# Attention scores and row maxima in five near-equal blocks of 460 or 462 columns instead of four of 512 and one of 256

## The reference

```python
attn = einsum('bqc,bkc->bqk', q * scale, k)          # 2304 x 2304 for each image and head
attn = attn + rel_h[..., :, None] + rel_w[..., None, :]   # relative position terms from q
attn = softmax(attn, axis=-1)
out = (attn @ v) @ proj_w + proj_b
x = x + out
```

## Time and profile before

| | |
|---|---|
| median of 3 runs | 6809.67 us (6804.43 to 6810.84) |
| profiled execution, span | 6801.4 us |
| PE busy / PEld busy | 6725.5 us (99%) / 4245.8 us (62%) |
| DVE busy | 5454.7 us (80%) |
| ACT busy | 4753.7 us (70%) |
| POOL busy | 938.1 us (14%) |
| DMA queue q1, share of the 16 engines | 68.9% |
| granted TensorE clock | full but for some slices' parts at the start and the end (2.4 GHz level) |

### The profile page before, as it was taken

One profiled execution on the slowest core, in us unless ns is written; L12 is line 12 of the kernel. 1 busy time (PEld: TensorE's weight loads), 2 busy tenths in 40 slices (PEclk: granted clock), 3 DMA queues, 4 the chain that ended last, 5 costly groups with the idle time before them and its releaser, 6 DMA issues.

```text
span 6801.4 us, 139326 instructions
## 1 busy us (share of the span) xinstructions
PE 6725.5 (99%) x53600; PEld 4245.8 (62%) x53600; DVE 5454.7 (80%) x9973; ACT 4753.7 (70%) x10225; POOL 938.1 (14%) x967
## 2 busy tenths in 40 slices
PE   7999999999999999999999999999999999999998
PEld 5666666666666666666665666666666666666664
DVE  7887888778887788877888778887888878888883
ACT  3776776767767777677776767767676676767775
POOL 2111010211112110121111210102101121101110
PEclk8999999999999999999999999999999999999999
DMA  6676676767677677667676766767677676777673
GB/s 164 148 156 152 137 160 138 163 151 142 152 144 168 144 143 156 149 158 149 142 155 149 158 143 143 161 145 166 140 144 157 147 165 138 143 152 156 144 154 88
DMA packets 306307, 1013.72 MB, mean 149 GB/s; under 512 B 107440, under 2 KB 196976, under 8 KB 215920
## 3 DMA queue, kind: packets, MB, share of 16 engines
q1 hardware_dynamic: 305648, 1004.81, 68.9%
HBM read 745.26 MB, written 255.69 MB: 147 GB/s over the span
## 4 chain that ended last, share of the span: by engine, by line
PE 96%; DMA 1%; DVE 1%; issue 0%; ACT 0%; SPq 0%; POOL 0%; DVEq 0%; ACTq 0%
PE work L805 30%; PE work L878 27%; PE work L796 27%; PE work L824 7%; PE work L843 3%; PE work L862 2%; PE work L851 1%; DMA moving<-rel_scratch 1%; DVE mpart L683 1%; PE work L830 0%; DVE xb L674 0%; ACT probs L561 0%; DMA back<-attention_scratch 0%; DVE hi L721 0%; PE work L835 0%
## 5 line engine op out<-in xcount | busy, mean ns | idle before, releaser
L683 DVE TENSOR_REDUCE mpart<-work 128x1 f32<-128x512 f32 (+1 forms) x8640 | 5088.7, 632 | 1079.7 <-PE work L805 1013.1
L561 ACT ACTIVATE probs<-work 128x512 f32<-128x512 f32 (+1 forms) x8640 | 4100.2, 564 | 866.6 <-PE work L796 852.1
L805 PE MATMUL work<-mkeys,hi 128*128 128x512 f32 (+1 forms) x8640 | 3404.1, 395 | 10.6 <-DVE mpart L683 8.8
L796 PE MATMUL work<-moving,keys 113*128 113x512 f32 (+1 forms) x8640 | 3299.9, 383 | 10.9 <-DMA moving<-rel_scratch 5.7
L805 PEld LDWEIGHTS work<-mkeys,hi 128*128 128x128 f32 x8640 | 1643.6, 190 | 622.4 <-DVE mpart L683 324.0
L878 PE MATMUL work<-probs,vall 128*17 128x288 f32 x27648 | 2013.1, 409 | 0.0
L796 PEld LDWEIGHTS work<-moving,keys 113*128 113x128 f32 x8640 | 1642.1, 190 | 362.3 <-ACT probs L561 39.2
L878 PEld LDWEIGHTS work<-probs,vall 128*17 128x17 f32 x27648 | 637.3, 96 | 846.8 <-ACT probs L561 358.3
L824 PEld LDWEIGHTS work<-image,tab 128*48 128x48 f32 x6912 | 401.6, 124 | 544.9 <-ACT probs L561 513.2
L490 POOL TENSOR_TENSOR full<-full,hi 128x384 f32<-128x384 f32 x576 | 583.5, 1016 | 938.7 <-DVE hi L721 937.6
L495 POOL TENSOR_TENSOR rden<-oraw,rden 128x576 f32<-128x576 f32 x96 | 137.1, 1428 | 3955.3 <-DMA rden<-inverse_scratch 3955.3
(11 more groups left out here) (42 smaller groups left out, 646.8 us busy)
## 6 DMA issues: line engine op xcount, KB each, us to landing
moving<-rel_scratch SPq DMA_DIRECT2D x1728, 144.0 KB
moving<-qk_scratch SPq DMA_DIRECT2D x288, 576.0 KB
rel_scratch<-hi SPq DMA_DIRECT2D x192, 432.0 KB, 5.7
rel_scratch<-full SPq DMA_DIRECT2D x192, 432.0 KB, 5.5
moving<-rel_scratch SPq DMA_DIRECT2D x288, 288.0 KB
image<-qk_scratch SPq DMA_DIRECT2D x384, 144.0 KB, 3.2
keys<-qk_scratch SPq DMA_DIRECT2D x192, 288.0 KB, 7.8
qk_scratch<-split_hi SPq DMA_DIRECT2D x144, 192.0 KB, 3.9
```

The lines of the kernel that those rows point to most:

```text
L561: act.activation(probs[:, tile % RING, lo:up], bank[:, 0:up - lo], ACT.Exp).then_inc(act_read, 1)
L683: dve.tensor_reduce(mpart[:, u % 2, q, m:m + 1], bank[:, 0:MSPLIT[m][1] - MSPLIT[m][0]], AX.X, ALU.max)\
L796: pe.matmul(bank[:, 0:up - lo], tile_of(keys[0:K_ROWS, u % 2, :], c, third), moving[0:K_ROWS, slot_of(u, third)[0], lo:up], start=True, st ...
L805: pe.matmul(bank[:, 0:up - lo], hi[:, u % 2, q * P:(q + 1) * P], mkeys[:, u % 2, lo:up], start=True, stop=True).then_inc(for_dve, 1)
```

## The change

The list of block borders is replaced. Everything that uses `SPLIT` and `MSPLIT` follows: the moving slices of L796 and L805, the widths of L561 and L683, nothing else. The first two blocks of the scores have 462 columns and the other three 460. Of the maxima, the first has 460, then come two of 462 and two of 460. The number of instructions, their order, the banks and the waits stay.

```diff
-SPLIT = [(512 * i, min(512 * i + 512, N)) for i in range(5)]
+EDGES = [0, 462, 924, 1384, 1844, N]
+SPLIT = list(zip(EDGES[:-1], EDGES[1:]))
 SB = len(SPLIT)
 MSPLIT = SPLIT[-1:] + SPLIT[:-1]
```

## The result

The changed kernel takes 6896.8 us (median of 4 runs, 6893.5 to 6898.2), the kernel before 6807.2 (4 runs, 6804.4 to 6810.8): ratio 1.013, 95% interval 1.0116 to 1.0143. It is slower by 90 us. That is under 2%, but clear of the noise. The forecast was 6905 us, from 6840 to 6935. The profiled spans are 6896.4 us after and 6801.4 before, 95.0 more; the forecast had +95 there. The profiled execution before took some 4 us less than the median of its kernel and the one after 1.4 more, so the spans differ by more than the medians.

The account below looks back on a forecast made before the run. TensorE's stream was taken as the bound, with DVE hidden one step behind. Plain tiles +0.06 us, statistics and v or fin tiles more: 99 us, less 4, gives +95 on 6801.4, plus 8.3 around the span: 6905 us, range 6840 to 6935.

Parts of the forecast that it names:

- That TensorE sets the tile, with DVE one step behind: Plain tile: TensorE's stream sets its length; DVE is a hidden second bound, max 1 released at 1.63, max 4 loading at 1.64.
- The step, 0.211: TensorE's time from one weight load to the next at 461 columns: 0.211 us, bounds 0.195 and 0.234.
- rival D: TensorE's step has a floor of 0.234 us: plain tile +0.13 us, some +205 us, 7015 us; chance 4%.
- rival A: Narrow blocks on TensorE step at 0.195 us: +0.02 to 0.03 us a tile, about 40 us, 6850 us; chance 8%.
- The release: DVE reads max 1 by 1.70 instead of 1.58, so max 4 loads at 1.75, score 4 at 1.86.
- Rival B: The later release by DVE isn't felt, TensorE's unmoved 2.31 for attend holds: 6810 us; chance 4%.
- rival C: Narrower step of 0.195 us and release not felt: -0.16 us a tile, some -250 us, 6560 us; chance 3%.
- The hidden part: Max 4's release 0.16 us late for its load; weight prefetch hides all but about 0.06 us per plain tile.
- Tiles with more: Tiles with extra work: statistics +0.34 us each, v or fin without mt +0.047, qk or mt zero.
- The sum: Seven stages of 12.5 us, last stage 10.9, first stage +0.7: 99 us, less 4 for absorbed waits: +95 us.
- the busy sums of DVE and ACT: Sign in the profile after: busy sums of both engines stay within 0.5%.
- over 1500 waits: Sign in the profile after: L805 weight-load waits on DVE grow from 729 to over 1500, short ones.

Follow-up runs that it names:

- run 1: Kernel before with only scores and exponentials in blocks of 460 and 462 columns, maxima kept at 256 first, then four of 512: 6826.2 us, ratio 1.0028.
- run 2: Kernel before with only the maxima in near-equal blocks, 460 first; scores kept at four of 512 and one of 256: 6834.7 us, ratio 1.0039.
- run 4: Kernel before with four blocks of 480 columns and one of 384, the 384 first among the maxima: 6828.5 us, ratio 1.0034.
- run 5: Changed kernel with DVE reducing only the first 230 of max 0's 460 columns, all else as is: 6807.9 us, ratio 1.0002 to the kernel before.
- run 3: Kernel before, same widths in another order: maxima 512 four times then 256, scores 256 first then 512 four times: 6965.8 us, ratio 1.0235.

## Why the prediction was right

*That TensorE sets the tile, with DVE one step behind.* Right. Runs 1, 2, 4 and 5 each have TensorE's blocks narrowed or DVE's widened without the meeting of the two, and none costs more than 27 us.

*The step, 0.211.* Measured 0.212. The floor of 0.234 (rival D) and rival A's 0.195 are both out: steps in the changed kernel's tile, up to the load of max 3, are 0.21 to 0.22. The rule N / 2.4 + 2.5 ns of the Trainium skill ("TensorE: Matmul & The Clock Gate", section Back-to-back issue gap) is given there for an isolated matmul, which the prediction didn't say; the trace agrees with it at neither width (0.216 by the rule against 0.234 at 512 columns, 0.195 against 0.212 at 461). The 256-column step was taken as 0.117, half of 0.234. Over the plain tiles it is 0.122 before and 0.120 in run 3, so the line does not quite pass through the origin, and the line through 0.122 and 0.234 gives the measured 0.212.

*The release.* Every term stood: reductions 0.55 apart, 0.63 long, load 0.05 after the end of the reduction, the next load 0.11 after that. Over all waits for max 1 in tiles without v and fin the load follows 0.053 after the end of the reduction. The load of max 4 was forecast to 0.01 in the changed kernel and in runs 2 to 5, and to 0.02 in run 1. Rival B (release not felt) fell with the changed kernel, rival C (faster) with it.

*The hidden part.* 0.16 late, 0.06 paid. Run 2 shows the same lateness of release with nothing paid, so it is the difference to TensorE's arrival that counts, not the wait.

*Tiles with more.* Statistics +0.320 against 0.34. v and fin +0.037 and +0.042 against 0.047. qk and mt nothing, as said. Tile 1 of each unit, where ACT copies the sums, I had not treated apart; it grew by 0.073, and by run 5 that is ACT's and not DVE's. There the number fitted the other tiles by luck.

*The sum.* 99 less 4 against 95.0. It is better than its terms deserve: the first units won 2.7 us, which I had at zero, and the 4 us for absorption were a guess. The +0.7 for the first stage should have been 0.1 (ten tiles at 0.06 in place of 0.047). Nor do 8.3 us lie around the span: every execution on record has 1.7 to 1.9 there, and the rest of the 8.3 is that the profiled execution was faster than the median. Adding it only moved the forecast to +95 on the median 6809.67; the medians differ by 90.

*What was wrong.* I wrote that the busy sums of DVE and ACT would stay within 0.5%. DVE's fell by 2.3% and ACT's rose by 0.9%. The mean durations were right. The lengths of all reductions add up to 5456 us before and 5433 after. But busy time counts overlapping operations once, and reductions that stand in a queue overlap by some 0.08 (0.63 long, 0.55 apart), while ones that wait for TensorE don't. One more overlap a tile, that of max 0 with max 1, is most of the 123 us that DVE's busy time lost. So a falling busy time of DVE was the sign of a fuller DVE queue. I also read the 324 us of waits before as standing on DVE's late release in general: 255 us of them are the load of max 0 and only 29 that of max 4, so they said little about the bound that the change would meet. The forecast of over 1500 waits held; 1390 of the 1479 new ones are at max 4.

*What stays open.* In runs 1, 2 and 4 the plain tile is 8 to 11 ns above the kernel before, in run 5, with narrow blocks everywhere, 2. In run 4 the steps account for most of it: 0.221 at 480 columns and 0.179 at 384, in the mean of the plain tiles, make 2.125 us for the ten blocks, against 2.117 before. For runs 1 and 2 the same sum differs from that of before by 2 ns at most, and no run says where the rest comes from. And no run moves the statistics without changing how many stand in a tile.

## What to carry to other kernels

Where one engine is full and another feeds on it through a short ring of buffers, don't ask how much work the second has, but when it has read the buffer that the first wants next. Put the small block where the reader starts, and keep other work of the reader out of the stretch between it and the release that is needed first; the statistics cost 0.44 us a tile with one of them there, and nothing once they stood ahead of max 4. Equal blocks are not a neutral choice, and two edits that cost 18 and 27 us alone can cost 90 together.

## What the runs showed of the hardware

- The fp32r matmuls of this kernel, behind a load of 128 columns, step by 0.234 us at 512 columns, 0.221 at 480, 0.212 at 460 or 462, 0.179 at 384 and 0.120 to 0.122 at 256, at the full granted clock. A line through these is 0.44 to 0.45 ns a column and 5 to 9 ns besides. The page of the Trainium skill "TensorE: Matmul & The Clock Gate", section Back-to-back issue gap, gives N / 2.4 + 2.5 ns for an isolated matmul; the steps here are above that at every width (0.234 against 0.216 at 512 columns).
- A weight load of 128 columns takes 0.19 in its row, but the next one follows after 0.11. A load that is released late costs only what goes beyond that: in run 2 the load of max 4 came 0.09 after the matmul of score 3 began, and the load of score 4 stood within 0.01 of where the steps alone put it; in the changed kernel it came 0.16 late and the tile lost 0.06.
- On DVE, reductions from PSUM in a queue start 0.60 apart at 512 columns and 0.55 at 460, with lengths of 0.68 and 0.63.
- Cutting a normalisation of 2304 columns on DVE into six of 384 made it hold DVE for 2.3 us in place of 1.39: a piece has 0.472 us in its row and holds DVE for about 0.39, the whole has 1.47 in its row.
